# Two head groups in one bank, a projection by even and odd dimensions, bf16 counts and a gate in two parts

## The chip, the cores and the metric
The kernel is one program on one core of a Trainium2 chip. The core has five engines that run their own instruction streams and meet at semaphores: TensorE (PE, matrix products), VectorE (DVE), ScalarE (ACT), GpSimd (POOL), and SyncE (SP), which here only issues DMAs. The metric is the device time of one execution in microseconds (us); a kernel's time is the median of its runs.

## The reference
One transformer layer on x of 8 batches x 512 rows x 128 values, all float32. First causal attention with 16 heads of 8 values and rotary position embedding, then a layernorm, then a mixture of 8 experts with 2 of them for each row plus one shared expert, then a second layernorm.

```
q, k, v = x @ Wq, x @ Wk, x @ Wv                # 128 x 128 each, 16 heads of 8
q, k = rope(q), rope(k)                         # (even, odd) pairs turned by the row's angle
attn = softmax(where(causal, q @ k.T / sqrt(8), -inf))
x = layernorm(x + (attn @ v) @ Wo)
logits = x @ router_w.T + experts_bias          # 8 experts
rw, sel = top_k(logits, 2); rw = softmax(rw)
moe = sum over the 2 chosen e of rw * ((silu(x @ w1[e]) * (x @ w3[e])) @ w2[e])     # hidden 256
shared = (silu(x @ sw1) * (x @ sw3)) @ sw2
x = layernorm(x + moe + shared)
```

## The kernel before
The work of a batch (called s) is cut into parts, and each part is a small function for one engine. Names of parts are used below.

**Attention.** `x_T` transposes x. `project` makes q and k as columns of heads and dimensions (partitions) by rows (512). It makes each twice: once with the weights `wq_sb`, `wk_sb` and once with `wqr_sb`, `wkr_sb`, whose columns are exchanged within each even and odd pair. DVE multiplies the first by the cosines and the second by the signed sines (`rope_products`, line 1567), and the sum of both is the turned q or k (`rope_sum`, line 921, on POOL from batch 1 on). Each is then split into three bf16 parts (`rope`, `rest`, `low`: lines 1185, 926, 1190, 931; ACT makes the first two, POOL the differences), and all float32 scores come from bf16 products of these parts. `store_parts` (line 988, SP) writes the parts to `parts_scratch` in DRAM in two DMAs, one for q and one for k, and `stack` (line 946, seven DMAs for each half of the heads) reads them back so that one product of 64 rows holds all pairs of parts. Batch 0 goes straight from `parts` to `stack` (line 957, `first` on SP and `first_act` on ACT).

`max_pair` (PE) makes scores for the maxima, DVE takes row maxima (line 1578), `max_rows` puts them back into the stack in three parts (`maxima`, line 993, SP). `score_pair` (PE, line 1321 with the maxima's) makes the scores, ACT the exponentials (line 1166), POOL the causal mask (line 1100), and `values` (PE, line 1365) multiplies them with `va`, the values of each head with a one behind them and zeros up to 32 columns, so that each head's row sums come along. There are 40 score units for a batch, and four groups of four heads: each group's result fills a PSUM bank, 32 partitions for each head, and ACT copies it to `ot` (line 1205). `heads_T` (line 1376) transposes `ot` back to rows, for each 128 rows one bank with 16 heads of 32 columns, and DVE divides by the sums (lines 1598, 1603). `out_T`, `out`, `ln1` and `x1_T` end the attention.

**Router and experts.** `router` picks two experts for each row; `both` marks them. For each group of batches in `SORTED` ([[0], [1, 2], [3, 4], [5, 6]]), `count` (line 1417) counts rows for each expert, and `rank` (lines 1429 to 1436) gives every row its place in a table sorted by expert, by products of `both` with constant matrices of zeros and ones, in float32. POOL scatters the rows to DRAM (line 1112), SP loads them back in tiles of 128 rows of one expert, with that expert's weights (`w_tile`, line 1018, a ring of eight). A tile is `T` (transpose), `gate` (four products, line 1459), `tanh` on ACT (line 1233), `glu` on DVE (`gated`: line 1710 makes gate x (1 + tanh), the engine waits for its own result, line 1718 multiplies by the up half), `down` (line 1471), a copy and a store. POOL gathers the two results of each row (line 1122) and DVE adds them. The last batch isn't sorted: all experts are computed on all its rows (`dense_*`, lines 1481, 1724, 1729, 1488, 1734).

**Order.** No order is written by hand. Every part has a due time (`AT`, in score units from the start of its batch) and a shift by engine, kind and phase of the program (`LATER`, in nanoseconds of the plan). `plan()` runs through the parts with a table of costs (`COST`), takes for each free engine the ready part with the lowest due time, and gives each product one of the eight PSUM banks. What it writes down is a fixed order for each engine, SP included.

Of the kernel before, what the change touches and what calls it, by code (L numbers as in the profile page):

```python
# [15 lines left out]
P = 128  # L16
# [19 lines left out]
AT = dict(weight_ahead=76.6758, tables=4.6839, fill=-92.6537, fill_step=26.5101, routed0=9.7812, routed1=-2.4771,  # L36
# [6 lines left out]
          T=-0.828, tanh=18.0034, glu=-7.352, down=-59.9696, stored=-39.2754, weight_late=17.0329, gather=24.049,  # L43
# [3 lines left out]
          dense_glu=66.1028, dense_down=60.2332, dense_mix=-44.1709, dense_weight=-101.7562,  # L47
# [4 lines left out]
LATER = {("act", "T"): (-231.19, -197.78, -432.38, -591.81, -659.48, -656.25, -505.22, -392.93, -156.67, -102.89,  # L52
         31.91, -192.47),
         ("act", "dense_tanh"): (259.86, 5.55, 88.3, 123.29, -266.78, 26.21, -94.53, -202.83, -202.46, 138.49, 34.8,
         -229.97),
         ("act", "down"): (503.15, 706.19, 606.53, 390.33, 661.04, 699.08, 784.95, 610.94, 583.32, 497.16, 148.96,
         119.18),
         ("act", "first_act"): (-70.69, -58.42, -81.48, -18.87, -2.13, -35.69, 6.35, -32.88, -52.62, -44.48, -30.03,
         -39.96),
         ("act", "out"): (-104.34, -133.18, -41.26, -161.51, -421.54, -365.3, -241.8, -406.0, -137.51, -289.15,  # L60
         -455.62, -634.98),
         ("act", "rest"): (563.46, 474.34, 575.88, 648.42, 678.75, 782.97, 684.96, 602.59, 443.77, 699.44, 919.5,
         869.11),
         ("act", "rope"): (750.4, 545.93, 657.48, 630.81, 679.34, 897.36, 841.58, 452.68, 164.55, 40.16, 205.26,
         500.34),
         ("act", "scores"): (-68.14, -211.83, -260.51, -313.03, 34.72, 49.14, -169.89, -120.58, 7.02, 42.64, 10.39,
         -120.19),
         ("act", "store_last"): (-190.53, -428.62, -539.54, -595.05, -642.69, -729.75, -549.93, -352.31, -486.05,
         -638.07, -455.94, -794.17),
         ("act", "tanh"): (106.93, 217.14, -13.54, 135.93, 182.38, 56.59, 263.65, -173.33, 87.8, -61.02, 251.1,  # L70
         -234.57),
         ("act", "v"): (159.32, -35.26, -214.74, -12.42, -134.91, -462.18, -382.5, -87.94, -174.4, 503.86, 322.37,
         351.29),
         ("act", "values"): (-268.17, -117.23, -81.25, 129.78, -56.72, -170.37, -619.73, -885.2, -558.27, -432.32,
         -110.15, -277.99),
         ("act", "weights"): (467.09, 643.03, 533.41, 658.19, 610.98, 640.64, 611.9, 661.49, 818.7, 715.15, 559.19,
         561.71),
         ("act", "x1_T"): (-58.75, -154.64, -231.92, -60.5, -199.68, -405.28, -66.03, -197.9, -230.68, 85.57, 157.76,
         146.24),
         ("act", "x_T"): (-275.65, -360.9, -713.9, -811.1, -515.93, -447.8, -280.09, -34.25, -380.51, -634.02,  # L80
         -387.89, -235.42),
         ("dve", "combine"): (-282.31, -389.23, -338.48, -394.47, -522.2, -392.33, -705.48, -796.51, -705.2, -856.37,
         -751.29, -756.92),
         ("dve", "count"): (48.42, -395.46, -323.75, 36.16, -112.7, -117.92, -300.34, -30.19, -123.17, -111.65,
         -558.68, -668.74),
         ("dve", "dense_glu"): (421.55, 371.07, 621.0, 594.2, 592.78, 354.52, 61.08, 50.88, 500.37, 731.39, 570.48,
         622.62),
# [1783 lines left out]
```

## Time and profile before

| | |
|---|---|
| median of 3 runs | 580.99 us (580.41 to 583.55) |
| span of the profiled execution | 604.0 us |
| PE busy | 530.3 us, 88% |
| DVE busy | 487.5 us, 81% |
| ACT busy | 314.4 us, 52% |
| POOL busy | 309.0 us, 51% |
| mean granted TensorE clock | 0.935 |

The profiled execution has no time of its own in the results apart from its span, which is the time from its first to its last instruction. Busy times say what an engine did; which of them sets the end has to be read by stretch, from the waits and from the order in time.

### The profile page before, as it was taken

What the parts mean: (1) busy time and instruction counts of PE and PEld (TensorE: products, weight loads), DVE (VectorE), ACT (ScalarE), POOL (GpSimd) and SP (SyncE); (2) the same over time, 40 slices, a digit from 0 to 9 for tenths busy, and PEclk for the clock granted to TensorE, in tenths of its full rate; (3) what the DMA queues carried; (4) which work ended last, traced back from release to release, by engine and by line L of the source; (5) the groups of instructions that cost most, each with busy time, mean ns of one, the idle gap of its engine ahead of it and who ended that gap; (6) DMA issues with size and microseconds to landing.
All of it is one profiled execution on the core that took longest, in us unless ns stands there. A gap on an engine that the chain in (4) does not pass through costs nothing.

```text
span 604.0 us, 14723 instructions
## 1 busy us (share of the span) xinstructions
PE 530.3 (88%) x4350; PEld 350.6 (58%) x4350; DVE 487.5 (81%) x1981; ACT 314.4 (52%) x744; POOL 309.0 (51%) x517
## 2 busy tenths in 40 slices
PE   6868997988999999999999999999994997999941
PEld 3312354534665656656666777666873996885531
DVE  4797799978999899899899879879951766768883
ACT  3107665646766566667676555776660444532200
POOL 5216546566364466657873556547584324143531
PEclk9777799989999989999999799999997999999985
DMA  6573321265426256454674374643464499960111
GB/s 187 143 238 100 107 81 47 88 207 170 117 73 194 82 155 179 116 165 111 195 188 123 92 237 146 187 129 111 121 186 163 121 283 269 310 219 19 52 40 35
DMA packets 75279, 87.40 MB, mean 145 GB/s; under 512 B 9984, under 2 KB 57984, under 8 KB 75200
## 3 DMA queue, kind: packets, MB, share of 16 engines
q1 hardware_dynamic: 67824, 77.21, 43.5%
q0 software_dynamic: 3584, 7.35, 4.0%
q10 hardware_dynamic: 3792, 1.90, 1.1%
q8 instruction: 36, 0.59, 0.4%
q14 instruction: 43, 0.35, 0.2%
HBM read 64.28 MB, written 20.05 MB: 140 GB/s over the span
## 4 chain that ended last, share of the span: by engine, by line
PE 54%; DVE 14%; issue 9%; SPq 6%; DMA 5%; ACT 4%; another core or an unknown queue 4%; POOL 2%; ACTq 0%; DVEq 0%; POOLq 0%
PE ps L1459 14%; PE ps L1365 9%; PE ps L1321 9%; PE ps L1471 7%; DVE sums L1578 3%; PE ps L1376 3%; ACT probs L1166 2%; PE ps L1443 2%; PE ps L1481 1%; DVE acc L1758 1%; DMA stack<-mparts 1%; SPq L957 1%; POOL yg L1122 1%; PE ps L1307 1%
## 5 line engine op out<-in xcount | busy, mean ns | idle before, releaser
L1578 DVE CUSTOM_DVE_ANT_0 sums<-ps,mask_sb 128x384 bf16<-128x384 f32 (+3 forms) x512 | 218.2, 484 | 18.1 <-PE ps L1321 17.7
L1166 ACT ACTIVATE probs<-ps 128x512 f32<-128x512 f32 x320 | 170.8, 611 | 48.0 <-PE ps L1321 42.5
L1100 POOL TENSOR_SCALAR_AFFINE_SELECT probs<-probs 128x256 f32<-128x256 f32 (+1 forms) x320 | 113.6, 365 | 128.4 <-ACT probs L1166 121.1
L1321 PE MATMUL ps<-stack 64*128 64x256 bf16 (+3 forms) x1024 | 116.6, 311 | 14.6 <-DMA stack<-mparts 5.1
L1459 PE MATMUL ps<-xgT,w_tile 128*128 128x128 f32 x672 | 91.8, 283 | 3.9 <-ACT xgT L1227 1.6
L1459 PEld LDWEIGHTS ps<-xgT,w_tile 128*128 128x128 f32 x672 | 82.7, 195 | 10.5 <-issue 7.6
L1365 PE MATMUL ps<-probs,va 128*32 128x512 f32 (+3 forms) x1024 | 82.6, 466 | 3.3 <-POOL probs L1100 1.7
L1710 DVE SCALAR_TENSOR_TENSOR gate<-th,ps 128x256 f32<-128x256 f32 x116 | 48.5, 418 | 43.0 <-ACT th L1233 36.9
L1321 PEld LDWEIGHTS ps<-stack 64*128 64x128 bf16 x1024 | 41.4, 95 | 70.5 <-issue 16.1
L1122 POOL DMA_INDIRECT yg<-rows_out,slot x56 | 54.0, 963 | 55.0 <-DVE acc L1758 29.9
L1233 ACT ACTIVATE th<-ps 128x256 f32<-128x256 f32 x116 | 45.3, 391 | 48.4 <-PE ps L1459 38.6
L1365 PEld LDWEIGHTS ps<-probs,va 128*32 128x32 f32 x1024 | 32.9, 115 | 51.9 <-issue 40.4
L1112 POOL DMA_INDIRECT rows_in<-x,slot x56 | 55.4, 989 | 12.1 <-issue 11.2
L1205 ACT ACTIVATE ot<-ps 128x512 f32<-128x512 f32 x32 | 19.1, 597 | 72.6 <-PE ps L1365 58.1
L1471 PE MATMUL ps<-w_tile,hid 128*128 128x128 f32 x336 | 52.7, 285 | 3.8 <-DVE hid L1718 1.9
L1471 PEld LDWEIGHTS ps<-w_tile,hid 128*128 128x128 f32 x336 | 43.7, 192 | 10.7 <-issue 7.1
L1578 DVE DVE_READ_ACCUMULATOR2_ANT negmax<- 128x1 f32 x512 | 41.4, 81 | 0.0
L1718 DVE TENSOR_TENSOR hid<-gate,ps 128x256 f32<-128x256 f32 x84 | 35.3, 421 | 2.9
L1459 PE MATMUL ps<-x1T,w_shared 128*128 128x128 f32 x256 | 35.5, 285 | 0.1
L1132 POOL TENSOR_TENSOR acc<-x,y_shared 128x128 f32<-128x128 f32 x32 | 14.6, 461 | 38.2 <-ACT y_shared L1241 38.1
L1459 PEld LDWEIGHTS ps<-x1T,w_shared 128*128 128x128 f32 x256 | 31.8, 196 | 3.4 <-issue 1.9
L1246 ACT ACTIVATE y_routed<-ps 128x128 f32<-128x128 f32 x84 | 23.1, 282 | 19.2 <-PE ps L1471 12.2
(119 smaller groups left out, 702.5 us busy)
## 6 DMA issues: line engine op xcount, KB each, us to landing
w_tile<-in_experts SPq DMA_DIRECT2D x92, 384.0 KB
stack<-parts_scratch SPq DMA_DIRECT2D x98, 128.0 KB
parts_scratch<-parts SPq DMA_DIRECT2D x14, 384.0 KB
xg<-rows_in SPq DMA_DIRECT2D x18, 256.0 KB
rows_out<-y_routed SPq DMA_DIRECT2D x61, 64.0 KB
rows_in<-zeros SPq DMA_DIRECT2D x14, 192.0 KB, 3.9
x_t<-in_x SPq DMA_DIRECT2D x8, 256.0 KB, 3.6
x_r<-in_x SPq DMA_DIRECT2D x8, 256.0 KB
```

The source lines that it names most:

```text
L1100: pool.affine_select(out=area, in_=area, compare_op=ALU.is_ge, fill=0.0, base=0, pattern=pattern, channel_multiplier=-1).then_inc(masked, 1)
L1112: pool.indirect_dma_start(out=rows_in[g % 2], out_offset=bass.IndirectOffsetOnAxis(ap=slot[:, r, s, t:t + 1], axis=0), in_=x1[:, s % X1RIN ...
L1122: pool.indirect_dma_start(out=yg[:, t, r, :], out_offset=None, in_=rows_out[g % 2][0:TILES[g] * P, :], in_offset=bass.IndirectOffsetOnAxis ...
L1166: act.activation(probs[:, (s * NB + v) % PRING, :], bank("scores", s, v), ACT.Exp, scale=SCALE)\
L1233: act.activation(th[:, i % 2, :], bank("gate", i)[:, 0:2 * P], ACT.Tanh, scale=0.5).then_inc(th_done, 1)
L1321: return pe.matmul(into[:, at:at + width], here[:, stationary, at_s:at_s + P], here[:, moving, at_m:at_m + width], start=True, stop=True)
L1365: last = pe.matmul(bank("values", s, g)[32 * k:32 * k + 32, j * P:S], va[:, j, PER_PV * g + k, :], probs[:, (s * NB + v) % PRING, at:at + ...
L1459: last = pe.matmul(bank("gate", i)[:, j * P:(j + 1) * P], w[:, j * P:(j + 1) * P], moving, start=True, stop=True)
L1471: last = pe.matmul(bank("down", i)[:, 0:D], hid[:, i % HRING, half * P:(half + 1) * P], w[:, (4 + half) * P:(5 + half) * P], start=(half = ...
L1578: ins = dve.tensor_tensor_reduce(sums[:, use % 2, at:at + w], bank("max", s, u)[:, at:at + w], mask_sb[:, S - w:S], -1.0, 3.0e38, ALU.add, ...
L1710: link(dve.scalar_tensor_tensor(out=gate[:, i % 2, :], in0=th[:, i % 2, :], scalar=1.0, in1=both_halves[:, 0:2 * P], op0=ALU.add, op1=ALU. ...
L1718: dve.tensor_tensor(hid[:, i % HRING, :], gate[:, i % 2, :], both_halves[:, 2 * P:4 * P], ALU.mult)\
```

## The change
Five things change.

1. **Values.** `va` holds two heads in 48 columns: values and one at 0 to 8, the other head's at 32 to 40, zeros elsewhere. The first head's product reads columns 0 to 31, the second's columns 16 to 47, so that its result lies 16 partitions further on. Two head groups add up in one bank. ACT copies two banks for a batch instead of four, `heads_T` has half of its transposes and one bank for 256 rows, and DVE divides with one reciprocal and one product instead of two each. The rows of `wv` and `wo` are exchanged to match.
2. **Projection.** From batch 1 on the two products have all even dimensions of q and k (`halved[0]`) and all odd ones (`halved[1]`). DVE multiplies each by the cosines and by the sines, the latter with a minus for the odd ones. Batch 0 is made as before, and then SP loads new tables over the old ones (`turn`, four DMAs). The parts now lie by side and dimension, so `store_parts` has four DMAs of 64 KB for each of the three parts, and each part is stored when it is ready.
3. **Counts.** `both`, `padded` and the constant matrices are bf16. They hold small whole numbers only.
4. **Gate.** `glu` becomes `gated` and `glu`, two parts with their own places; the dense one too.
5. **Places.** All numbers in `LATER` are new, and some costs of the plan.

```diff
-            add(now + AT["store_parts"] + 0.01 * c, "store_parts", s, c)
+        for a in range(3 if s else 0):
+            add(now + AT["store_parts"] + 0.01 * a, "store_parts", s, a)
...
-LATER = {("act", "T"): (-231.19, -197.78, -432.38, -591.81, -659.48, -656.25, -505.22, -392.93, -156.67, -102.89,
+LATER = {("act", "T"): (-1315.33, -1821.62, -722.34, -979.12, -799.38, -1148.04, -763.48, -2008.15, -3885.33, 17.13,
...
-            def store_parts(s, c):
-                sp.wait_ge(part2, split_count(s, c))
-                sp.wait_ge(part1, split_count(s, c))
+            def store_parts(s, a):
+                sp.wait_ge((part0, part1, part2)[a], split_count(s, 2))
                 if s > 1:
                     for k in (2 * s - 2, 2 * s - 1):
                         sp.wait_ge(*stack_full(k))
-                sp.dma_start(scratch[c, 0:3, :, :].rearrange("a p n -> p a n"), parts[:, c, :, :]).then_inc(scr_out, 16)
+                for side in range(2):
+                    for c in range(2):
+                        rows = bass.AP(scratch.tensor, scratch[side, a, c * (H // 4), 0].offset,
+                                       [[2 * (H // 4) * S, P // 8], [S, H // 4], [1, S]])
+                        sp.dma_start(rows, parts[side * (P // 2):(side + 1) * (P // 2), c, a, :]).then_inc(scr_out, 16)
...
+            def turn_tables():
+                for c in range(2):
+                    for n in range(2):
+                        sp.wait_ge(*drained("project", 0, c, n))
+                for dst, src in ((cos_sb, turns[0]), (sin_sb, turns[1]), (wq_sb, halved[0]), (wk_sb, halved[1])):
+                    sp.dma_start(dst[:, :], src).then_inc(turned_in, 16)
...
             def project(s, c):
                 pe.wait_ge(*drained("x_T", s, 0))
-                for n, w in enumerate(((wq_sb, wqr_sb), (wk_sb, wkr_sb))[c]):
+                if s > 0:
+                    pe.wait_ge(turned_in, 64)
+                for n, w in enumerate(((wq_sb, wqr_sb), (wk_sb, wkr_sb))[c][0:products_of(s)]):
...
-                take("values", s, g)
+                into, second = bank("values", s, g // 2), g % 2
+                if not second:
+                    take("values", s, g // 2)
...
-                        last = pe.matmul(bank("values", s, g)[32 * k:32 * k + 32, j * P:S], va[:, j, PER_PV * g + k, :],
-                                         probs[:, (s * NB + v) % PRING, at:at + S - j * P], start=(j == 0), stop=(j == T - 1),
-                                         skip_group_check=True)
-                last.then_inc(full("values", s, g), 1)
+                        last = pe.matmul(into[32 * k:32 * k + 32, j * P:S],
+                                         va[:, j, PER_PV * (g // 2) + k, 16 * second:16 * second + 32],
+                                         probs[:, (s * NB + v) % PRING, at:at + S - j * P],
+                                         start=(j == 0 and not second), stop=(j == T - 1 and second == 1), skip_group_check=True)
+                last.then_inc(full("values", s, g // 2) if second else values_read, 1)
...
             def rope_products(s, c):
                 if s > 0:
                     dve.wait_ge(part2, split_count(s - 1, 0))
+                    dve.wait_ge(turned_in, 64)
+                    dve.wait_ge(*filled("project", s, c, 0))
+                    own = bank("project", s, c, 0)
+                    dve.tensor_tensor(qk[:, c, :], own, cos_sb[:, :], ALU.mult)
+                    if c == 0:
+                        ins = dve.tensor_tensor(rest[:, 1, :], own, sin_sb[:, :], ALU.mult)
+                    else:
+                        ins = dve.scalar_tensor_tensor(out=rest[:, 0, :], in0=own, scalar=-1.0, in1=sin_sb[:, :],
+                                                       op0=ALU.mult, op1=ALU.mult)
+                    ins.then_inc(free("project", s, c, 0), 1)
+                    return
...
             def gated(i):
                 dve.wait_ge(th_done, i + 1)
-                both_halves = bank("gate", i)
-                link(dve.scalar_tensor_tensor(out=gate[:, i % 2, :], in0=th[:, i % 2, :], scalar=1.0, in1=both_halves[:, 0:2 * P],
-                                              op0=ALU.add, op1=ALU.mult), gate_done, i + 1)
+                if i >= 2:
+                    dve.wait_ge(*drained("gate", i - 2))
+                dve.scalar_tensor_tensor(out=gate[:, i % 2, :], in0=th[:, i % 2, :], scalar=1.0, in1=bank("gate", i)[:, 0:2 * P],
+                                         op0=ALU.add, op1=ALU.mult).then_inc(gate_done, 1)
+
+            def hidden(i):
+                dve.wait_ge(gate_done, i + 1)
```

Three places show what the new numbers and parts do to the order. The first is PE at the transposes of a batch's values in the middle of the program (batch 5), before the change; `ot` holds the weighted values, `hid` is a tile's hidden layer.

```order
L1365 MATMUL ps<-probs,va 32x128 x4
L1471 MATMUL ps<-w_tile,hid 128x128 x4
L1376 MATMUL ps<-ident_sb,ot 128x128 x8
L1321 MATMUL ps<-stack 128x384
L1321 MATMUL ps<-stack 128x128
L1321 MATMUL ps<-stack 128x384
L1321 MATMUL ps<-stack 128x128
L1376 MATMUL ps<-ident_sb,ot 128x128 x8
L1321 MATMUL ps<-stack 128x256 x4
```

The same place behind the change (line 1446 is the transposes, 1387 the stack's products, 1454 the transposes of `on`):

```order
L1433 MATMUL ps<-probs,va 32x128 x4
L1540 MATMUL ps<-w_tile,hid 128x128 x4
L1446 MATMUL ps<-ident_sb,ot 128x128 x4
L1387 MATMUL ps<-stack 128x256 x4
L1446 MATMUL ps<-ident_sb,ot 128x128 x4
L1387 MATMUL ps<-stack 128x512 x2
L1528 MATMUL ps<-xgT,w_tile 128x128 x4
L1454 MATMUL ps<-ident_sb,on 128x128 x4
```

Each row of eight transposes is now a row of four; what stands around them is much the same.

The second is SP around the stores of the parts (`parts_scratch`) of batch 4, before the change; `expert` is the read of a tile's expert number, which goes ahead of the load of its weights.

```order
L993 DMA stack<-mparts 2x16x128 x3
L1017 TENSOR_LOAD expert
L1017 ISA x2
L1018 ISA
L1018 DMA w_tile<-in_experts 128x768
L967 DMA rows_out<-y_routed 128x128
L988 DMA parts_scratch<-parts 128x3x512 x2
L1017 TENSOR_LOAD expert
L1017 ISA x2
L1018 ISA
L1018 DMA w_tile<-in_experts 128x768
L967 DMA rows_out<-y_routed 128x128
```

And behind the change (line 1039 is the stores, 1044 the maxima's parts, 1015 the store of a tile's rows):

```order
L1044 DMA stack<-mparts 2x16x128 x3
L994 DMA stack<-parts_scratch 16x2x2048 x7
L1068 TENSOR_LOAD expert
L1068 ISA x2
L1069 ISA
L1069 DMA w_tile<-in_experts 128x768
L1039 DMA parts_scratch<-parts 16x4x512 x12
L1015 DMA rows_out<-y_routed 128x128 x2
L1068 TENSOR_LOAD expert
L1068 ISA x2
```

Two stores became twelve in a row. In four of the seven batches all twelve stand together; in the others the plan puts other DMAs between them.

The third is PE at the last group of weighted values of the last batch, before the change (line 1443 transposes a tile's rows, 1459 is its gate):

```order
L1365 MATMUL ps<-probs,va 32x128 x4
L1471 MATMUL ps<-w_tile,hid 128x128 x2
L1443 MATMUL ps<-ident_sb,xg 128x128
L1459 MATMUL ps<-xgT,w_tile 128x128 x4
L1376 MATMUL ps<-ident_sb,ot 128x128 x8
L1443 MATMUL ps<-ident_sb,xg 128x128
L1459 MATMUL ps<-x1T,w_shared 128x128 x4
```

And behind it:

```order
L1433 MATMUL ps<-probs,va 32x128 x4
L1540 MATMUL ps<-w_tile,hid 128x128 x4
L1446 MATMUL ps<-ident_sb,ot 128x128 x4
L1540 MATMUL ps<-w_tile,hid 128x128 x2
L1512 MATMUL ps<-ident_sb,xg 128x128
L1446 MATMUL ps<-ident_sb,ot 128x128 x4
L1528 MATMUL ps<-xgT,w_tile 128x128 x8
```

Ahead of this point stand 208 of the 336 gate products of routed tiles before the change and 256 behind it, four for a tile: 12 tiles moved from behind the last attention to ahead of its end. In DVE's order 60 of the 116 gate steps have other instructions between their two halves; before, none had.

## Rows read from the trace of the kernel before

**Rows 1.** The page, busy us, share of the span and instructions of each engine.

```profile
PE 530.3 (88%) x4350; PEld 350.6 (58%) x4350; DVE 487.5 (81%) x1981; ACT 314.4 (52%) x744; POOL 309.0 (51%) x517
```

**Rows 2.** Busy us of each engine in four stretches, clock, DMA.

```profile
0.00:150.00 150.00, 122.53 (x880) 55.69 (x880) 122.05 (x523) 73.81 (x140) 74.58 (x134) 0.87 0.45 136
150.00:350.00 200.00, 192.99 (x1721) 127.01 (x1725) 184.77 (x800) 129.84 (x299) 116.87 (x206) 0.97 0.49 139
350.00:450.00 100.00, 98.09 (x961) 72.47 (x954) 81.51 (x348) 66.64 (x171) 59.96 (x113) 1.00 0.54 155
450.00:604.00 154.00, 116.74 (x794) 95.41 (x792) 99.18 (x315) 44.16 (x137) 57.59 (x66) 0.90 0.50 154
```

**Rows 3.** Waits of PE: for whom, us in total, times, longest us.

```profile
PE ps L1376 <- ACT ot L1205: 9.1, 3, 7.2
...
PE ps L1321 <- DMA stack<-parts_scratch: 1.1, 1, 1.1
```

**Rows 4.** Order in time: start us, us, engine, line; idle before and releaser.

```profile
464.26 0.60 ACT L1205 ACTIVATE ot<-ps 128x512 f32<-128x512 f32 x1 [11.30 <-remote]
...
588.03 3.75 PE L1488 MATMUL ps<-w_tile,probs 128*128 128x128 f32 x16 [7.81 <-issue]
```

**Rows 5.** Order in time, PE, two projections.

```profile
191.91 1.12 PE L1307 MATMUL ps<-xT,wk_sb 128*128 128x512 f32 x2
...
193.73 0.27 PE L1352 MATMUL ps<-ident_sb,negmax 128*32 128x128 f32 x1
```

**Rows 6.** Order in time, PE, transposes.

```profile
249.35 1.09 PE L1376 MATMUL ps<-ident_sb,ot 128*128 128x128 f32 x8
...
252.87 0.63 PE L1385 MATMUL ps<-ident_sb,on 128*128 128x128 f32 x4 [0.32 <-DVE on L1603]
```

**Rows 7.** Order in time, PE: stack, counts, and a block of ranks.

```profile
197.88 1.04 PE L1321 MATMUL ps<-stack 64*128 64x512 bf16 x12 [1.05 <-DMA stack<-parts_scratch]
...
205.91 0.55 PE L1417 MATMUL ps<-consts_sb,both 128*8 128x1 f32 x16
...
331.56 0.41 PE L1429 MATMUL ps<-both,consts_sb 128*128 128x64 f32 x2 [0.34 <-ACT probs L1166]
...
333.98 1.36 PE L1321 MATMUL ps<-stack 64*128 64x512 bf16 x8
```

**Rows 8.** Order in time, DVE, the division by the row sums.

```profile
250.22 0.53 DVE L1598 RECIPROCAL rden<-ps 128x16 f32<-128x16 f32 x2
250.78 0.49 DVE L1603 TENSOR_TENSOR on<-ps,rden 128x128 f32<-128x128 f32 x2
```

**Rows 9.** Groups by shape, count | busy us, mean ns | idle before, releaser.

```profile
L1710 DVE SCALAR_TENSOR_TENSOR gate<-th,ps 128x256 f32<-128x256 f32 x116 | 48.5, 418 | 43.0 <-ACT th L1233 36.9 <-issue 5.4
...
L1718 DVE TENSOR_TENSOR hid<-gate,ps 128x256 f32<-128x256 f32 x84 | 35.3, 421 | 2.9
...
L1603 DVE TENSOR_TENSOR on<-ps,rden 128x128 f32<-128x128 f32 x32 | 7.8, 286 | 0.5
```

**Rows 10.** Stack loads of 64 KB: issue ns min/median/max, first and last start.

```profile
L957 SPq DMA_DIRECT2D stack<-parts x18: 532/544/625, 11.4 to 25.4; - x18
```

**Rows 11.** Order in time, batch 4's parts; last row from the chain.

```profile
174.13 1.06 ACT L1185 ACTIVATE parts<-qk 128x1024 bf16<-128x1024 f32 x1 [0.51 <-POOL qk L921]
...
180.46 2.14 POOL L931 TENSOR_TENSOR parts<-rest,parts 128x1024 bf16<-128x1024 f32 x1 [1.20 <-ACT parts L1190]
...
183.52 0.92 SPq L988 DMA_DIRECT2D parts_scratch<-parts  x2
...
184.07 5.24 DMA parts_scratch<-parts
```

**Rows 12.** Order in time, SP and ACT, first loads of the stack.

```profile
11.44 1.21 SPq L957 DMA_DIRECT2D stack<-parts  x2
...
18.27 7.65 SPq L957 DMA_DIRECT2D stack<-parts  x12
...
27.45 1.06 ACT L1185 ACTIVATE parts<-qk 128x1024 bf16<-128x1024 f32 x1 [10.36 <-DMA stack<-parts]
```

More of the change, by code:

```diff
@@ L197 @@
 COST = dict(
-    pe=dict(x_T=(480, 660), project=(1800, 1970), v=(930, 1080), max_rows=(110, 290), values=(2300, 2390), heads_T=(890, 1060),
-            out_T=(490, 630), out=(970, 1160), x1_T=(490, 660), router=(880, 1060), count=(470, 560), rank=(2450, 2550),
+    pe=dict(x_T=(480, 660), project=(1800, 1970), v=(930, 1080), max_rows=(110, 290), values=(2300, 2390), heads_T=(450, 620),
+            out_T=(490, 630), out=(970, 1160), x1_T=(490, 660), router=(880, 1060), count=(220, 310), rank=(620, 720),
@@ L206 @@
+             weights=(490, 600), count=(560, 660), rank=(1480, 1590), gated=(335, 455), glu=(335, 430), dense_gated=(600, 720), dense_glu=(600, 700), mix=(1140, 1260), mix_end=(280, 400), combine=(2340, 2340),
              ln2_stats=(1390, 1510), ln2=(1030, 1140)),
@@ L298, in build_block @@
             add(now + AT["values"] + UPG * (g + 1), "values", s, g)
+        for h in range(GROUPS // 2):
+            add(now + AT["values"] + UPG * (2 * h + 2), "values_out", s, h)
         for pair in range(2):
@@ L413, in build_block @@
         add(at, "gate", i)
-        for kind in ("tanh", "glu", "down"):
+        for kind in ("tanh", "gated", "glu", "down"):
             add(at + AT[kind], kind, i)
@@ L438, in uses_of @@
         engine, reader = READER.get(kind, ("act", kind))
+        if kind == "values":
+            both = (key[0], key[1] // 2)
+            return [] if key[1] % 2 else [((kind, *both), (engine, reader, *both))]
         if kind in ("score_pair", "max_pair"):
@@ L441, in uses_of @@
             return [((reader, *unit), (engine, reader, *unit)) for unit in units]
-        if kind in ("project", "heads_T", "dense_gate"):
+        if kind == "dense_gate":
+            return [((kind, *key, n), ("dve", ("dense_gated", "dense_glu")[n], *key)) for n in range(2)]
+        if kind == "project" and key[0] > 0:
+            return [((kind, *key, 0), (engine, reader, *key))]
+        if kind == "project":
             return [((kind, *key, n), (engine, reader, *key)) for n in range(2)]
@@ L611, in needs @@
         if kind == "store_parts":
-            own = split("low", s)
+            own = [[("act", "rope", s, 2)], [("act", "rest", s, 2)], split("low", s)][key[1]]
             return own + [n for half in range(2) if s > 1 for n in stacked_by(s - 1, half)]
@@ L1069, in _ @@
                     store_out(*key)
+                elif kind == "turn":
+                    turn_tables()
                 elif kind == "tables":
@@ L1271, in _ @@
                     store_v(key[0])
-                elif kind == "values":
+                elif kind == "values_out":
                     values_out(*key)
```

475 lines of the change are left out of this document (263 added, 212 removed).

## The prediction

> **What bounds the kernel now.** I read the page first, then the busy times by stretch, then the waits of PE, then the order of time at the places that the change touches. The page's first line says that PE is busy 88% of the span and DVE 81% [rows 1]. The stretches say where each of them binds [rows 2]: from 0 to 150 us both are at about 122 of 150 us, so the first batches still wait for each other; from 150 to 350 us PE has 193.0 of 200 us and DVE 184.8; from 350 to 450 us PE has 98.1 of 100 and DVE only 81.5; behind 450 us PE has 117 of 154. So PE sets the pace from 150 to 450 us, and DVE is 4 points behind it for the first two thirds of that. PE's own waits are small: the longest is for the copies of the weighted values, 9.1 us in 3 times with 7.2 us in one of them, and a wait for the stack's loads comes once, 1.1 us [rows 3].
>
> The long one is a stall of its own kind: ACT does nothing for 11.30 us before the copy at 464.26 us, and PE idles 7.81 us before 588.03 us with nothing ahead of it that the profile shows [rows 4]. The profiled execution has a span of 604.0 us and the runs a median of 580.99 us, so 23 us are in this execution that are not in the timed ones; the two stalls make 19 of them. I make the sum as a difference and take it from both: I do not count on the stalls to go or to stay.
>
> **What the change takes off PE.**
> Projections: two products of 512 columns take PE from 191.91 to 193.73 us, 0.91 us each [rows 5]. From batch 1 on each batch has two instead of four: 7 x 2 x 0.91 = 12.7 us.
> Transposes of the values: a row of eight has 1.09 us, four of the same kind from `on` have 0.63 us [rows 6]. Sixteen groups of eight become groups of four: 16 x 0.46 = 7.4 us.
> Ranks: the block of 20 matmuls of a group of two batches takes 2.42 us (331.56 to 333.98), 0.12 us each [rows 7]; the group of one batch has 12 of them, about 1.5 us. In bf16 each float32 product becomes one instruction instead of two, so 10 and 6. No row has a bf16 matmul of this width; the nearest is the stack's, twelve in 1.04 us, 0.09 us each at up to 512 columns [rows 7]. Between half of the present time for each (0.06) and that 0.09 I take 0.07, since the width here is under 65: 0.7 us for a block, a gain of 1.7 three times and 1.0 once, 6.1 us. By the ends it would be 6.5 and 5.4.
> Counts: 16 have 0.55 us [rows 7]. A group has 8 or 16 of them, 56 in all; half go, 0.9 us.
> The weighted values keep their number and widths; only the bank is shared.
> Sum for PE: 12.7 + 7.4 + 6.1 + 0.9 = 27.1 us.
>
> **What it takes off the others.** DVE: two reciprocals and two products of a pair take 1.05 us (250.22 to 251.27) [rows 8]. They become one reciprocal, some 0.26, and one product over 256 columns, 0.42 by the gate's row of that width [rows 9]: 0.35 us saved, 16 times, 5.6 us. The split of the gate removes the wait between its two halves: 84 of the second halves have 2.9 us of idle time before them, 0.035 us each [rows 9], and neighbours that need no wait overlap: two products of 0.286 us stand in 0.49 us [rows 8, 9], 0.08 us less. Of 116 steps and 16 dense ones, sixty steps have other work between the halves now, so I take 4 us, between 0 and 132 x (0.035 + 0.08) = 15. The Trainium skill says otherwise (VectorE: DVE Perf Modes, "The DRAIN you can't avoid"): an op does not start until the pipe is empty and "the semaphore costs nothing extra". By that rule the split gives 0 and the forecast would be 2 us later; the overlap of 0.08 us in this trace speaks against it.
> ACT: 16 copies of 0.60 us go [rows 4], 9.6 us. ACT is at 52% [rows 1], so I count them at nothing.
> The products on DVE stay four for a batch, and the one that negates is of a kind that takes 0.418 us where the plain one takes 0.421 us at equal width [rows 9]: nothing. The smaller bf16 tiles of the router are a few instructions: nothing.
>
> **What it adds.** SP issues 12 stores of 64 KB for a batch instead of 2 of 384 KB. Issues of 64 KB took 0.544 us [rows 10], and the two old stores 0.92 us together [rows 11], so SP spends 6.5 us for a batch instead of 0.9. The Trainium skill (DMA: Bandwidth & Descriptors, "Bandwidth") has a rule against this: batch transfers, small ones are dominated by their fixed part. On the path the trace speaks for the change: the last part was ready at 182.60 us, both stores were issued by 184.44, and they landed at 189.31 us, 5.24 us after they began [rows 11]. Now two thirds of the bytes leave before that, and behind the last part stand 4 x 0.544 = 2.2 us of issues and the landing of one of 64 KB, which I put at half of the 5.24 us at most: 4.8 us instead of 6.7. PE waited for this path once, for 1.1 us [rows 3], so it has slack: I count 0, between +2 (four issues where there were two) and -1.1.
> Four more loads stand in front of the first loads of the stack, and SP waits ahead of them for DVE's last product of batch 0, while its first stack load went out at 11.44 us. Four issues take at most 4 x 0.54 = 2.2 us. The second half of the stack is a row of 12 issues from 18.27 to 25.92 us, and ACT's first copy of batch 1 waits for its landing until 27.45 us [rows 12]; both move by up to that. Whether batch 1 is early enough to take it I can't read: 0 to +2.2 us, I take +1.
> A bank is held from the first group's matmuls to the copy behind the second, instead of the copy alone; projections and transposes need one bank less each. These offset: 0, between +3 and -3.
>
> **The sum by stretch.** From 0 to 150 us lie the products of batches 1 to 3, the transposes of batches 0 and 1 and the first rank: 8.5 us of PE. PE and DVE alternate there with 18% idle each; I take 0.4 of it, 3.4 us, and give 1 us back to the four loads: 2.4. From 150 to 350 us lie 4 x 1.82 + 3 x 0.92 + 2 x 1.95 = 13.9 us of PE. That leaves PE with 179 us, and DVE with 184.8 less about 5.5, also 179. The busier of two that are level will not be held at 96.5%; at 95% the stretch takes 188.6 us, and I take 10.5 us. From 350 to 450 us lie 3.8 us and DVE has room: 3.8. Behind 450 us 0.9 us. The new places add one thing that I can read: at the last group of weighted values 256 of 336 gate matmuls of routed rows are done instead of 208, twelve tiles that no longer stand in the stretch of which PE has 37 us idle, 19 of them in the two stalls. A sixth of the other 18, 3 us: the last 15 us of the span are the end of one chain, and no tile lies there. Sum: 2.4 + 10.5 + 3.8 + 0.9 + 3 = 20.6 us. The profile of the changed kernel would have a span near 583 us with the same stalls, and the runs 580.99 - 20.6 = 560 us.
>
> **Rivals.**
> PE gets its whole gain. Its share in the two bound stretches is 96.5% and 98%, and DVE sheds 10 us of its own. Then 27 us and 3 us at the end come off: 551 us. Against it: 18% idle in the first 150 us.
> DVE takes over. DVE keeps its 92.4% of the stretch from 150 to 350 us, 179 / 0.924 = 194 us, a gain of 6; with 1.5 from the start and 3.5 and 0.9 behind, 12 us: 569 us. For it: DVE's share is high while PE is full.
> SP holds the rest up, and the kernel is slower. In four of seven batches all twelve stores stand in one row, and the first waits for the first part: from 175.19 us (174.13 + 1.06) to 182.60 us SP would have been held for 7.4 us [rows 11], with weight tiles, stored rows and the maxima's rows queued behind. If scores or gates wait out 7 us of this six times, 42 us are lost and 20.6 gained: 602 us; at two thirds of that, 588. It decides from 20.6 / 6 = 3.4 us for a batch. Against it: weights stand in a ring of eight, and the maxima's rows stand before or behind the block, not in it.
> The table of new places gives all of it back through a poorer mix of work: 581 us. I see no row for it.
>
> **Chances.** Forecast 0.50, whole gain 0.20, DVE 0.18, no change 0.05, slower 0.07. The time is that of the forecast, 560 us, its own range 554 to 566. The range for 8 in 10 reaches into both neighbours: 548 to 574 us. A difference under 0.5% (3 us) can't be told from none here: faster 0.88, same 0.05, slower 0.07.
>
> **What would show it.** Products: 18 instead of 32, PE's instructions down from 4350 by about 28 + 64 + 64, PE busy near 503 us. Right if PE stays over 95% from 150 to 430 us and DVE rises to about 94%. DVE as the bound would show as more waits of PE's stack matmuls for the maxima, now 4.5 us. SP's hold would show as waits of PE for stack loads, of gates for weights, and SP waiting for ACT's and POOL's parts by over 5 us for a batch. The forecast is wrong if the span falls under 10 us although PE sheds 27.

## The result

The changed kernel takes 584.8 us (median of 20 runs, 580.11 to 590.51), the kernel before 581.67 us (20 runs beside them, 578.25 to 587.09). The ratio is 1.0052, 95% interval 1.0027 to 1.0076: 0.5% or 3 us slower, with 1 just outside the interval. I had forecast 560 us, and 548 to 574 us for 8 in 10. The profiled execution has a span of 583.0 us and 584.74 us of its own.

The page of the changed kernel, the line of [rows 1]:

```profile
PE 514.1 (88%) x4194; PEld 335.5 (58%) x4194; DVE 478.7 (82%) x1949; ACT 308.5 (53%) x728; POOL 308.5 (53%) x518
```

The instructions are gone as forecast, 156 on PE. [Rows 1] come from an execution with a span of 604.0 us, so I took the kernel before once more (`before_again`: 583.79 us, span 582.0). The 11.30 us stall of [rows 4] isn't there; the one ahead of L1488 is, with 6.95 us. The stretches of that execution, columns as in [rows 2]:

```profile
0.00:150.00 150.00, 124.12 (x898) 56.78 (x902) 124.41 (x531) 76.43 (x144) 75.67 (x137) 0.87 0.47 141
150.00:350.00 200.00, 194.43 (x1764) 128.46 (x1754) 185.25 (x801) 129.28 (x299) 117.06 (x204) 0.98 0.49 142
350.00:450.00 100.00, 98.30 (x966) 73.22 (x965) 79.82 (x339) 68.19 (x176) 63.21 (x116) 1.00 0.53 159
450.00:582.00 132.00, 107.74 (x733) 88.36 (x731) 96.47 (x311) 41.88 (x128) 53.12 (x61) 0.94 0.53 166
```

And of the changed kernel:

```profile
0.00:150.00 150.00, 120.75 (x855) 56.06 (x856) 124.67 (x521) 72.31 (x137) 77.45 (x137) 0.85 0.47 144
150.00:350.00 200.00, 185.91 (x1671) 120.62 (x1671) 179.75 (x768) 125.11 (x289) 112.76 (x200) 0.97 0.48 142
350.00:450.00 100.00, 97.04 (x879) 70.27 (x879) 80.58 (x356) 66.59 (x173) 60.52 (x111) 0.97 0.56 161
450.00:583.00 133.00, 110.36 (x794) 88.53 (x793) 93.69 (x307) 44.49 (x132) 57.74 (x73) 0.94 0.52 165
```

From 150 to 350 us PE's busy time went down by 8.5 us and DVE's by 5.5, so both engines idle more. A stretch is a piece of the clock and not of the work, so the work has to be dated by itself: the first row maxima of batches 4 to 7 start at 194.8, 243.7, 305.6 and 362.0 us in `before_again` and at 193.8, 248.2, 314.9 and 371.3 us here: 1 us earlier at first and 9 us later in the end, although each batch's attention has less work for PE. PE's total fell by 10.5 us only (524.6 to 514.1), and it idles for 68.9 instead of 57.4 us. PE's groups before (`before_again`; columns as in [rows 9]):

```profile
L1321 PE MATMUL ps<-stack 64*128 64x256 bf16 (+3 forms) x1024 | 116.4, 311 | 13.3 <-DMA stack<-mparts 5.8 <-DVE negmax L1578 4.0 <-DVE mparts L1592 1.7
L1376 PE MATMUL ps<-ident_sb,ot 128*128 128x128 f32 x128 | 17.2, 277 | 0.0
...
L1307 PE MATMUL ps<-xT,wkr_sb 128*128 128x512 f32 x16 | 9.5, 683 | 0.0
...
L1307 PE MATMUL ps<-xT,wqr_sb 128*128 128x512 f32 x16 | 8.2, 592 | 0.0
...
L1431 PE MATMUL ps<-both,consts_sb 128*128 128x24 f32 (+6 forms) x48 | 5.9, 268 | 0.0
```

and of the changed kernel:

```profile
L1387 PE MATMUL ps<-stack 64*128 64x512 bf16 (+3 forms) x1024 | 125.3, 316 | 16.4 <-DMA stack<-mparts 5.2 <-DVE mparts L1672 3.0 <-DVE negmax L1658 2.8
...
L1446 PE MATMUL ps<-ident_sb,ot 128*128 128x128 f32 x64 | 10.1, 280 | 0.0
...
L1500 PE MATMUL ps<-both,consts_sb 128*128 128x24 bf16 (+6 forms) x24 | 1.2, 176 | 0.0
...
L1373 PE MATMUL ps<-xT,wkr_sb 128*128 128x512 f32 x2 | 1.0, 592 | 0.0
```

Projections (all four groups) 37.0 to 22.7, transposes 17.2 to 10.1, counts and ranks (five groups) 12.5 to 4.8: 29.1 us off, where I had 27.1. A group's busy time counts in full what overlaps a neighbouring group; with every moment of PE counted once it is 27.5 us. But the 1024 matmuls of the stack, which nobody touched, are busy for 8.9 us more, and everything outside the edited groups, the stack included, for 17.0 us more (27.5 less 10.5). Some of that is the clock. The mean granted clock is 0.948 in `before_again` and 0.932 here; over 19 executions of each it is 0.945 and 0.932, which is 64 and 79 us at 1.2 GHz (twice the missing share of the span). One place shows how it falls, the changed kernel around 142 us:

```profile
128.00:142.00 14.00, 13.44 (x124) 6.85 (x118) 12.83 (x48) 9.35 (x18) 8.53 (x18) 1.00 0.51 156
142.00:145.20 3.20, 0.51 (x9) 0.22 (x5) 3.20 (x8) 1.57 (x3) 2.61 (x4) 0.93 0.01 4
145.20:155.00 9.80, 9.51 (x48) 6.04 (x52) 7.97 (x44) 5.58 (x12) 3.92 (x5) 0.50 0.28 79
```

PE waits 2.69 us for the row maxima there, and the next 9.8 us of work run at half clock. The kernel before has no such wait at 142 us (3.09 of 3.2 us busy) and a clock of 1.00 behind it.

### The profile page after: what moved, and what is told of

It is laid out like the page before. It is cut to its first block, busy times and chain, and to the rows that moved or that the text cites. A ratio compares the mean times of both kernels' runs of the same rounds, so it can differ in the third digit from the quotient of the medians.

```text
span 583.0 us, 14526 instructions
## 1 busy us (share of the span) xinstructions
PE 514.1 (88%) x4194; PEld 335.5 (58%) x4194; DVE 478.7 (82%) x1949; ACT 308.5 (53%) x728; POOL 308.5 (53%) x518
## 4 chain that ended last, share of the span: by engine, by line
PE 51%; DVE 19%; issue 9%; SPq 7%; ACT 4%; POOL 4%; DMA 4%; DVEq 0%; POOLq 0%; ACTq 0%
PE ps L1528 15%; PE ps L1540 9%; PE ps L1387 8%; PE ps L1433 8%; DVE sums L1658 5%; ACT probs L1228 3%; POOL yg L1184 3%; SPq L1039 2%; DVE acc L1842 2%; PE ps L1512 1%; SPq L994 1%; DMA stack<-parts_scratch 1%; PE ps L1476 1%; DVE x L1695 1%; DVE y_sb L1695 1%
## 5 line engine op out<-in xcount | busy, mean ns | idle before, releaser
L1387 PE MATMUL ps<-stack 64*128 64x512 bf16 (+3 forms) x1024 | 125.3, 316 | 16.4 <-DMA stack<-mparts 5.2
L1528 PE MATMUL ps<-xgT,w_tile 128*128 128x128 f32 x672 | 92.1, 284 | 1.7 <-DVE negmax L1658 0.7
L1387 PEld LDWEIGHTS ps<-stack 64*128 64x128 bf16 x1024 | 44.9, 96 | 77.4 <-DVE negmax L1658 18.1
L1433 PE MATMUL ps<-probs,va 128*32 128x512 f32 (+3 forms) x1024 | 80.9, 458 | 3.6 <-POOL probs L1162 3.2
L1540 PE MATMUL ps<-w_tile,hid 128*128 128x128 f32 x336 | 53.4, 287 | 3.6 <-DVE hid L1799 3.5
L1528 PE MATMUL ps<-x1T,w_shared 128*128 128x128 f32 x256 | 37.7, 294 | 1.5 <-ACT probs L1228 0.7
L969 POOL TENSOR_TENSOR qk<-qk,rest 128x1024 f32<-128x1024 f32 x7 | 16.5, 2359 | 24.0 <-DVE rest L1639 24.0
```

Source lines behind the costliest of these rows:

```text
L1387: return pe.matmul(into[:, at:at + width], here[:, stationary, at_s:at_s + P], here[:, moving, at_m:at_m + width], start=True, stop=True)
L1433: last = pe.matmul(into[32 * k:32 * k + 32, j * P:S], va[:, j, PER_PV * (g // 2) + k, 16 * second:16 * second + 32], probs[:, (s * NB + v) ...
L1528: last = pe.matmul(bank("gate", i)[:, j * P:(j + 1) * P], w[:, j * P:(j + 1) * P], moving, start=True, stop=True)
L1540: last = pe.matmul(bank("down", i)[:, 0:D], hid[:, i % HRING, half * P:(half + 1) * P], w[:, (4 + half) * P:(5 + half) * P], start=(half = ...
```

## The experiments

Each run's ratio is to the kernel before, run beside it on the same chip; 1% is 5.8 us. The changed kernel's own ratio is 1.0052, so its variants are compared with that.

**Places against edits.** The old table in the changed kernel, the new one in the kernel before:

```diff
-LATER = {("act", "T"): (-1315.33, ...   # changed kernel
+LATER = {("act", "T"): (-231.19, ...
```

> The changed kernel with the table of places of the kernel before (the gate's two halves both take the old gate's number, the turn loads get none). Theory T1, the new table gives back what the other edits bring: 560 to 568 us. Theory T2, TensorE's work is no longer what sets the pace and the waits among DVE, ACT and PE swallow what it sheds, whatever the order: 576 to 586 us. Theory T3, PE binds, but something that the change adds (12 stores, turn loads, a bank held longer) costs about 20 us: 580 to 588 us, with longer waits of PE for the stack or SP waiting for parts.

> The kernel before with the new table of places (the gate, still one step, takes the number of its last half), nothing else changed. T1: the table is poorer by about 20 us, so 596 to 604 us. T2 and T3: the table is worth little, 578 to 587 us. If the table only fits the changed kernel, this one is slower even though the table is good there; then old_places tells.

Measured: 602.02 us, ratio 1.0313 (1.0253 to 1.0374), and 638.62 us, ratio 1.0940 (1.0857 to 1.1022), both slower than every theory had said. With the old table the changed code is 15 us slower still (5.6 us of it a wait of PE for the turn loads, which the old table gives no number). Each table fits its own kernel alone. T1 falls in the form that the old table would do better. Whether some third table would do better for the changed code, these runs don't say.

**More and less work in a fixed order.** These change no instruction's place. The fence gives each edit in short, several lines left out.

```diff
 # pe_refill (also each transpose of ot twice)
+for again in range(1 if s == 0 else 2):
     last = pe.matmul(bank("project", s, c, n), w[:, :], xT[:, s % 2, :], ...)
 # pe_less_on_before (with the change's bf16 counts and ranks); pe_less_on_after: the one product
+w, moving = (bf16 view of w, of xT)      # s > 0
 # dve_less_on_after, both_less_on_before: products of q and k, s > 0
-dve.tensor_tensor(qk[:, c, :], own, cos_sb[:, :], ALU.mult)
+dve.tensor_tensor(qk[:, c, 0:KS], own[:, 0:KS], cos_sb[:, 0:KS], ALU.mult)
 # dve_more_on_after
+for again in range(2): dve.tensor_tensor(spare[:, 2 * c + again, :], own, cos_sb[:, :], ALU.mult)
 # act_more_on_after
+act.activation(spare[:, h, :], bank("values", s, h), ACT.Copy)
```

> The changed kernel in exactly its own order, but each projection of batches 1 to 7 is issued twice into the same bank (14 more products of 0.91 us) and each transpose of the weighted values twice (64 more, 9 us): 21.7 us of PE work come back and nothing else changes. T1 and T3, PE binds: 603 to 607 us. T2, PE has slack that swallows most of it: 585 to 594 us.

> The kernel before in exactly its own order, with less PE work: router counts and ranks in bf16 (7.7 us off by the two traces) and the second product of q and k of batches 1 to 7 in bf16, so that it is approximate (the row of the stack's bf16 matmuls says about 0.25 instead of 0.91 us, 9 us off): about 17 us of PE work less. T1 and T3, PE binds: 565 to 569 us. T2: 574 to 580 us.

> The kernel before, unchanged: one more profile, since the one at hand has 19 us in two stalls (11.30 us ahead of the copy at 464.26 us, 7.81 us before 588.03 us). If the stalls belong to that one execution, span 578 to 583 us and the stretch behind 450 us like the changed kernel's; if they belong to the kernel, they stand here again.

> The changed kernel in its own order, with the 28 products of q and k of batches 1 to 7 on DVE cut from 512 to 64 columns (most of q and k is then left out): 28 times about 0.46 us = 13 us of DVE work off, nothing off PE. Theory T4, PE and DVE both stand at their limit from 100 to 350 us and hand the work to each other, so that each has a part of the path: 573 to 579 us, a gain of half the work or more. Theory T2b, a third thing sets the pace (latency of ACT and POOL's softmax chain, DMA): 582 to 586 us. If DVE alone sets the pace: 570 to 573 us.

> The changed kernel in its own order, with two more products of 512 columns for each of q and k in batches 1 to 7, into a tile that nobody reads: 28 times 0.68 = 19 us more DVE work. T4: 593 to 600 us (60 to 80% of it, as pe_refill had 12.6 of 21.7). T2b: 585 to 590 us. DVE alone: 602 to 604 us.

> The kernel before in its own order, with pe_less_on_before's edits (about 17 us less PE work, which by themselves gained nothing: 584.3 against 583.2 us) and the 28 products of q and k on DVE cut to 64 columns as well (13 us less DVE work; most of q and k is left out). T4: what PE shed shows once DVE sheds as well, 568 to 574 us, more than the 13 us of DVE would bring alone only if it falls under 570. T2b: 580 to 585 us. DVE alone: 570 to 573 us.

> The changed kernel in its own order, with each of the 16 copies of weighted values on ACT done twice (the first into a tile nobody reads): 16 times 0.6 = 9.6 us of ACT work come back, as much as the change took off ACT. If ACT has slack as its 53% says: 584 to 586 us. If the chain from scores over ACT and POOL to the weighted values sets the pace (T2b): 590 to 594 us.

> The changed kernel in its own order, with the product of q and k of batches 1 to 7 in bf16 (approximate): 14 times 0.6 = 8.6 us less PE work. In the order of the kernel before, 17 us less PE work gave nothing, while here 21.7 us more cost 12.6. If PE's work moves the time here in both directions at 58%: 579 to 581 us. If relief is worth nothing, only load costs: 584 to 586 us.

In the table a run's parent is the kernel that it was made from, and the last column is the difference of the two ratios, times 583 us; it is uncertain by 2 to 4 us.

| run | work changed, by its rows | median us | ratio (95%) | against its parent |
|---|---|---|---|---|
| pe_refill | PE +19.4 | 597.38 | 1.0215 (1.0156-1.0273) | +9.5 us |
| dve_more_on_after | DVE +17.9 | 599.60 | 1.0320 (1.0275-1.0365) | +15.6 |
| act_more_on_after | ACT +9.6 | 587.42 | 1.0069 (1.0038-1.0101) | +1.0 |
| dve_less_on_after | DVE -13.0 | 580.85 | 0.9961 (0.9937-0.9984) | -5.3 |
| pe_less_on_after | PE about -12 | 585.66 | 1.0079 (1.0048-1.0111) | +1.6 |
| pe_less_on_before | PE -16.4 | 584.29 | 1.0040 (1.0000-1.0079) | +2.3 |
| both_less_on_before | PE -16.4, DVE -13 | 583.25 | 1.0005 (0.9974-1.0036) | +0.3 |

Load on PE costs half of what it is, load on DVE 87%; relief of PE gives nothing in either order. Relief of DVE gives 40% in one order (5.3 us, 3.3 to 7.3); in the other, with PE relieved too, `both_less_on_before` is 2.0 us under `pe_less_on_before` (-5.0 to +0.9), which does not tell a small gain from none. T1 and T3 are out (they asked 565 to 569 of `pe_less_on_before`). T2 holds for relief, though its own 574 to 580 was too low. `pe_refill`, `dve_less_on_after` and `act_more_on_after` fell between the ranges of their theories. T4's reason for it, that DVE holds PE's gain back until it is relieved as well, is refuted by `both_less_on_before` (568 to 574 expected). ACT's copies do not set the pace.

The lower clock can't have eaten the relief of PE: over its 10 executions `pe_less_on_before` has a mean clock of 0.939 against 0.944 of the kernel before beside it, some 6 us more at half clock. If PE's work takes twice as long there, that is 3 us of the 16.4.

Where the relief goes can be read from `pe_less_on_before`, in the order of the kernel before, from 150 to 350 us:

```profile
150.00:350.00 200.00, 186.93 (x1716) 121.64 (x1708) 186.54 (x800) 129.76 (x299) 117.28 (x204) 0.99 0.49 142
```

PE is busy for 7.5 us less than in `before_again` (194.43), DVE for 1.3 more, and nothing comes earlier by more than 1 us: the first row maxima of batches 4 to 7 start at 195.1, 243.4, 305.8 and 361.7 us, where `before_again` has 194.8, 243.7, 305.6 and 362.0. All of PE's waits in that stretch sum to 12.1 us instead of 4.3: 7.8 us more. So the shed work turned into waits one for one. Who ends them (for whom, us, times, longest):

```profile
PE ps L1329 <- DVE negmax L1586: 2.5, 3, 1.9
PE ps L1451 <- DVE negmax L1586: 1.5, 6, 0.3
PE ps L1451 <- DVE rest L1575: 1.3, 1, 1.3
PE ps L1479 <- DVE hid L1726: 1.0, 3, 0.5
PE ps L1329 <- DMA stack<-parts_scratch: 0.9, 1, 0.9
```

No single one: row maxima, the products of q and k, the gate, a load of the stack. With DVE's products cut as well:

```profile
150.00:350.00 200.00, 188.66 (x1699) 123.35 (x1697) 179.47 (x795) 128.66 (x297) 117.29 (x204) 0.96 0.50 143
```

DVE sheds 5.8 us there and waits 6.1 more (9.7 to 15.8), and PE is busy for longer than in `pe_less_on_before` at a lower clock, 0.96 against 0.99.

**The clock.** Does the lower clock take what PE sheds? I filled PE's longest early waits with matmuls of zeros (the fence shows two of the four places; the others are ahead of batch 1's x and of batch 0's first scores):

```diff
+def warm(into, n):
+    for _ in range(n): pe.matmul(into, idle[:, 0:P], idle[:, :], start=True, stop=True)
 ...
+warm(bank("max_rows", s, half), {(0, 0): 5, (2, 1): 8}.get((s, half), 0))
 pe.wait_ge(*drained("max", s, half * NB // 2 + NB // 2 - 1))
```

> The changed kernel in its own order, with 33 matmuls of zeros (bf16, 512 columns) at the four places where PE waits longest before 150 us: 12 ahead of batch 1's x (PE waits 5.7 us there), 5 and 8 ahead of the first row maxima and of batch 0's first scores (3.0 and 4.1 us), 8 ahead of the row maxima at 142 us (2.7 us). In every trace so far PE falls to the lower clock right behind such a wait: the changed kernel has 65 us at half clock ahead of 560 us, the kernel before 44. Theory T5, the clock takes a part of what PE shed: fewer than 50 us at half clock before 560 us, and the time falls by 3 to 8 us, to 577 to 582 us. If the clock follows something else, or batch 0's start is paced by loads anyway: 584 to 587 us, the added matmuls costing up to 2 us.

Measured: 588.53 us, ratio 1.0095 (1.0051 to 1.0140), 2.5 us above the changed kernel (-0.5 to +5.5). Its mean clock was 0.933 against 0.932: the filling hardly raised it, and it delayed batch 0's first scores (ACT's first exponentials start at 48.5 instead of 45.5 us). So this run does not test the cause well. What remains is a correlation: over the 19 executions of each kernel the time rises by 0.34 us (before) and 0.12 us (changed) for each us at half clock (each with a standard error of 0.07 to 0.08), so 15 us more of it go with some 2 to 5 us of time. The Trainium skill (TensorE: Matmul & The Clock Gate, "Terms") puts the penalty at the throttled time times the missing half, which makes an estimate of 7.5 us for these 15; the runs show less. The mean clocks of the fixed-order runs go with PE's work only in part: 0.920 for `pe_less_on_after`, 0.939 for `pe_refill` and 0.932 for their parent, 0.939 for `pe_less_on_before` and 0.933 for `both_less_on_before` against 0.944 and 0.945 beside them. But `dve_more_on_after`, in which PE has the same work and waits longer, has 0.916, the lowest of these.

**The order as a draw.** The table multiplied by random factors. The fence says in short what was done, for a draw within 1%; the third draw of the changed kernel has 5%, the three of the kernel before 2%, 1% and 5%.

```diff
+LATER = {k: tuple(x * (1 + uniform(-0.01, 0.01)) for x in v) for k, v in LATER.items()}
```

> The changed kernel, every number of its table of places changed by a random factor within 1%. The same instructions; 2,100 of the 3,151 steps stand at another place of their engine's list, from the first seventh of PE's list on. Theory T6, the time of a code is drawn anew with each order, with a spread as large as the gain I looked for: between 575 and 605 us, off the changed kernel's 585 by 5 us or more. If the order matters only through what the planner weighs: within 3 us of 585.

> As other_order_1 with another draw of the factors within 1%: 1,677 of the 3,151 steps stand elsewhere, from the first third of PE's list on. T6: 575 to 605 us and off both the changed kernel and other_order_1. Otherwise within 3 us of 585.

> The changed kernel with a third draw of its table, each number changed by a random factor within 5% (1,287 of 3,151 steps stand elsewhere, from the middle of PE's list on). The first two draws gave 595.2 and 590.2 against 585 of the table as it stands. T6: 586 to 600 us.

> The kernel before, each number of its table changed by a random factor within 2%; 746 steps stand elsewhere, from the first third of PE's list on. If the lighter code of the change is worth its 20 us in an order that nobody picked, and the kernel before only stands level because its own order is a lucky one: 605 to 615 us, 15 to 20 above the draws of the changed kernel (595, 590). If the lighter code is worth nothing in any order: 588 to 598 us like those draws.

> As before_other_order_1 with factors within 1%; 1,062 steps stand elsewhere, from the middle of PE's list on. Lighter code worth 20 us: 605 to 615 us; worth nothing: 588 to 598 us.

> As before_other_order_1 with factors within 5%; 901 steps stand elsewhere, from the first third of PE's list on. Lighter code worth 20 us: 605 to 615 us; worth nothing: 588 to 598 us.

| order | changed kernel | kernel before |
|---|---|---|
| its own | 1.0052 | 1 |
| draw 1 | 1.0179 (1.0126-1.0232) | 1.0143 (1.0074-1.0212) |
| draw 2 | 1.0118 (1.0076-1.0160) | 1.0031 (0.9994-1.0069) |
| draw 3 | 1.0036 (0.9997-1.0074) | 1.0050 (1.0013-1.0088) |

T6 holds in part: a change of 1% in the table moves the time by up to 7 us, but draw 3 of the changed kernel is level with its own order, outside T6's 586 to 600. Draws 2 and 3 of the kernel before (584.0 and 587.5 us) lie under both ranges that I had given. In neither kernel is a draw clearly faster than its own order, so each order is a good one of its kind, and the kernel before isn't lucky by the 15 to 20 us asked for. The mean of the three draws is 1.0111 for the lighter code and 1.0075 for the heavier one. Three draws with steps of 4 us don't separate these, but they exclude a gain of 20 us (3.4%) for the lighter code in orders near these two. The comparison isn't quite even: the changed kernel's numbers are several times larger, and 1,287 to 2,100 of its steps moved, against 746 to 1,062.

**The stores.**

```diff
-for side in range(2):                      # for each of the three parts
-    for c in range(2):
-        sp.dma_start(rows, parts[side * (P // 2):(side + 1) * (P // 2), c, a, :])
+for c in range(2 if a == 2 else 0):
+    sp.dma_start(scratch[c, 0:3, :, :].rearrange("a p n -> p a n"), parts[:, c, :, :])
```

> The changed kernel in its own order, with two stores of 384 KB for a batch behind the last part, as before, in place of 12 of 64 KB (the same bytes leave, but heads land in each other's places, so the attention is that of mixed heads). SP's queue stands on the chain of waits of the changed kernel from 29 to 38 us and from 64.7 to 73.7 us, twelve stores each time. Theory T7, the stores hold the start of the program up: 6 to 12 us off, 573 to 579 us. If the lockstep of PE and DVE hides them, as every relief so far was hidden: 583 to 586 us.

Measured: 582.66 us, ratio 1.0013 (0.9984 to 1.0042), 2.3 us (0.1 to 4.5) under the changed kernel. T7 is refuted in its size. The chain of waits had suggested more (start us, us, what):

```profile
64.73 0.56 SPq L1039
...
71.08 0.60 SPq L1039
...
71.72 2.00 DMA parts_scratch<-parts
```

Twelve issues in a row on the chain, but what they delay would have been late anyway: in both kernels SP issues the first maxima's rows at the same time, 41.80 us here and 41.93 us with two stores. A chain names one path and not what removing it gives, and here another was close behind.

No run with the whole computation in it was faster than the kernel before.

## Why the prediction was wrong

**PE bounds the kernel from 150 to 450 us.** This is the step that failed, in the sum by stretch: "From 150 to 350 us lie [...] 13.9 us of PE [...] I take 10.5 us". I read a share of 96.5% as a pace that PE sets. It says only that PE's queue was hardly ever short of work in that order. `pe_less_on_before` shows 16.4 us less work for no gain (+2.3 us, 0 to 4.6), at the very projections and ranks from which I counted 19.7 of the 27.1 us; `pe_less_on_after` shows 12 us for none, and the stretch shows waits that grew by what the work fell. The transposes, 7.4 us, were not tried by themselves. So it is shown that PE's work at these places was worth nothing; why is not shown. In that stretch DVE is busy for 185.3 us and waits for 9.7 in `before_again`, PE for 194.4 and 4.3. That the two hand the work back and forth, so that an engine relieved at one place waits at the next, is what the waits suggest, but with both relieved the time is 583.25 us and not the 568 to 574 that this asked for, so it can't be the whole reason.

The signs named in the prediction came out against it: from 150 to 430 us PE is at 94% and not over 95%, DVE at 89% and not 94%, and the time did not fall although PE shed its 27 us. One slip in the sum changes nothing: 200 less 188.6 us is 11.4 and not 10.5.

**PE sheds 27.1 us.** Right: 27.5, each moment counted once. PE busy near 503 us did not follow from it (514.1), since the rest of PE's work took 17.0 us more.

**DVE sheds 5.6 and 4 us.** The division's two groups fell from 14.7 to 12.5 us, 2.2 and not 5.6: the reciprocal over both tiles takes 0.356 us, I had 0.26. Its rows and those of the gate after:

```profile
L1787 DVE SCALAR_TENSOR_TENSOR gate<-th,ps 128x256 f32<-128x256 f32 x116 | 47.6, 416 | 28.7 <-ACT th L1297 28.2
...
L1799 DVE TENSOR_TENSOR hid<-gate,ps 128x256 f32<-128x256 f32 x84 | 34.4, 416 | 1.2
...
L1679 DVE TENSOR_TENSOR on<-ps,rden 128x256 f32<-128x256 f32 x16 | 6.8, 424 | 0.6
...
L1678 DVE RECIPROCAL rden<-ps 128x32 f32<-128x32 f32 x16 | 5.7, 356 | 8.5 <-PE ps L1446 8.2
```

The idle time ahead of the gate's second halves went from 4.0 to 1.5 us (84 and 32 of them). Their groups' busy time hardly fell, but it counts overlaps in full, and the overlap of 0.08 us with a neighbour was what I had counted on. With each moment of DVE counted once, the gate's three groups fell from 91.9 to 85.0 us. That makes 9.4 us for the split, more than twice the 4 I took, inside my 0 to 15, and not the 0 of the rule that the prediction quotes. So DVE shed more than I had counted there, and the kernel still did not gain.

**ACT's 9.6 us count nothing.** Right: 1.0 us (-1.3 to 3.3) when put back.

**SP's stores count 0, between -1.1 and +2.** Measured 2.3 (0.1 to 4.5): just over the upper end. **The four turn loads +1.** The second row of first loads begins at 19.06 instead of 18.27 us, and ACT's first copy of batch 1 at 28.17 instead of 27.45 [rows 12]. But `before_again`, without any turn loads, has 19.11 and 28.21 us, so these 0.7 us lie between two executions of one kernel, and the loads cost nothing that can be seen.

**Twelve tiles ahead of the last attention's end, 3 us.** They moved, and PE's last weighted values start at 475.9 instead of 448.0 us; 107 us follow instead of 134. The tail is shorter by 27 us, the part ahead longer by 28. Twelve tiles are some 24 us of PE work (the three groups of routed rows, 92.1 + 53.4 + 21.5 us, are 84 tiles). I had counted what they free behind the attention and nothing for the room that they take ahead of it. The part ahead, `before_again` and then the changed kernel:

```profile
0.00:448.00 448.00, 414.85 (x3600) 256.65 (x3604) 389.48 (x1670) 272.85 (x613) 254.55 (x455) 0.95 0.49 145
0.00:475.90 475.90, 429.59 (x3652) 269.21 (x3652) 399.44 (x1681) 277.27 (x639) 267.37 (x472) 0.93 0.51 152
```

Of the 28 us PE is busy for 14.7 and idle for 13.2. The tiles came in and about as much work went out, so had PE set the pace, this part would have stayed near 448 us.

**The rivals.** "DVE takes over" (569 us) was nearer than the forecast but still had 12 us of gain where there was none: it let PE's relief run out at DVE's bound, while nothing was to be had from the start. "SP holds the rest up" fails by the run above. "The table gives it back", which I gave 0.05 and had no row for, had nearly the right time, 581, by luck: its reason, a poorer table, is not what the runs show, since the old table is 15 us worse for this code. I had no rival in which PE's relief is worth nothing.

**What stays open.** What sets the pace when PE and DVE are both relieved. The lower clock goes with some 2 to 5 us of it, shown only as a correlation; PE's waits for rows that go over SP and a DMA, and the small idle times between instructions, are candidates that I did not separate. The 8.9 us more in the stack's matmuls are explained only in part. Whether another order would let the lighter code gain was not tried beyond the neighbours of the two tables.

## What to carry to other kernels

Where two engines are both over 90% busy in a written order, a busy share is no bound: before shedding work, double it and cut it at one place in the fixed order, and price the edit by what the cut gives, which here was nothing while added work cost half of itself. A chain of waits or a busy share says where time was spent, not what removing it would give. And where a planner writes the order, compare codes over several orders, since a 1% change of its table moved the time by more than this change did.

## What the runs showed of the hardware

A wait of PE of 2.69 us was followed by 9.8 us at half clock, and the changed kernel, with 27.5 us less PE work and longer waits, had a lower mean clock (0.945 to 0.932 over 19 executions each). A float32 product of 512 columns with a bf16 result takes DVE 0.681 us, as long as with a float32 result (0.678); cut to 64 columns it takes 0.22 us. A reciprocal of 32 columns takes 0.356 us against 0.238 for 16.
